# Attention of the first block: a second product of keys and queries in place of transposed scores, with the distances added by the vector engine

## The chip, the cores and the metric

The kernel runs on one NeuronCore of one Trainium2 chip. The metric is the time of one execution on the device in microseconds. TensorE (PE) multiplies into PSUM; VectorE (DVE), ScalarE (ACT) and GpSimd (POOL) work element by element, GpSimd on SBUF alone here; SyncE (SP) issues most DMAs. Each engine works through its own queue in order, and semaphores tie the queues together.

## What is computed

Input x is 8 sequences of 512 tokens with 256 features. Two transformer blocks follow each other; all is float32. Cut to what matters here:

```python
# first block, for each of 8 sequences; H = 16 heads of 16 features
h = layer_norm(x) * (1 + scale) + shift           # from gelu(cond) @ Wt
q, k, v = split(h @ Wqkv)
scores = q @ k.T / 4 - torus_dist * torus_scale[head]
attn = softmax(where(pad, NEG_INF, scores))
x = x + (attn @ v) @ Wout
x = x + gelu(layer_norm(x) @ W1) @ W2
# second block: masked attention without distances, gated by a conditioning vector, and an MLP
```

torus_dist is one 512 x 512 matrix for all sequences, torus_scale one number a head.

## The kernel before

There are 16 passes n: 0 to 7 are the first block's sequences (B = 8), 8 to 15 the second block's. A pass does the attention of sequence n and, between its steps, the dense work of its neighbours: t1 and qk (transposes and projection) of sequence n + 1, v of n itself, and t3, wout, t2, up and down (the rest of the block) of n - 1. The table FIRST says at which step which of these pieces stands, FIRST_DOWN the same for the 32 chunks of the down projection. Three PSUM banks serve the pieces in turn.

The attention of the first block has 32 units of one head and one half (256) of the queries. For a unit u at step k = u (37 steps a pass):

- TensorE, `scores` (line 829): two matmuls of 97 rows, 128 queries by 512 keys. The 97 rows are three terms of 16 split features for two heads, and a mask row. Each goes to one of two score banks.
- VectorE, `shift_scores` (line 1338): adds the scaled distances `bias` to the bank, writes the result to `shifted` and reduces its minimum to `row_max` (signs are turned, so that the minimum stands for the maximum). An instruction that reads the accumulator follows each.
- `bias`, the distances times the head's scale, is made by GpSimd (line 590) for three units in four and by ScalarE (line 1054) for one.
- GpSimd, `subtract_max` (line 597): two subtractions on `shifted`.
- TensorE, `turn_unit` (line 841), two steps later: eight 128x128 transposes, so that keys lie on partitions.
- ScalarE, `exps` (line 1065): two exponentials from PSUM into `probs`.
- TensorE, `attend` (line 856), once for four units: 16 products of probs with `v_ext` (values and a column of ones), 32 instructions.
- ScalarE `take_out` (line 1073), TensorE `to_tokens` (line 865), VectorE `divide` (lines 1359, 1363): the head's output is turned back to tokens and divided by its sum.

A step's order is written out by hand: on TensorE scores, attend, transposes, to_tokens, dense pieces, down chunks; on VectorE division, reductions, dense pieces of the step before, norms. SyncE stores the split q and k to HBM (`store_half`) and loads them back in the layout of the score matmul (`load_group`, a group of four heads in four DMAs). The second block (`pair_scores_of`, `turned_scores_of`) already forms its scores a second time with the maximum in four extra rows; this stays as it is.

## Time and profile before

| | us |
|---|---|
| median of three runs | 1467.23 (1465.11 to 1467.56) |
| the profiled execution, its own time | 1468.33 |
| its span, first to last instruction | 1466.5 |
| TensorE busy | 1307.7 (89%) |
| VectorE busy | 813.6 (55%) |
| ScalarE busy | 771.1 (53%) |
| GpSimd busy | 734.4 (50%) |
| first score product | at 43.8 |
| first score reduction of passes 0, 1, 4, 7 | at 44.78, 129.08, 452.18, 776.21 |
| first reduction of the second block | at 905.23 |

Busy is the time in which an engine has an instruction under way; what stands beside a group of instructions as idle is how long the engine stood still just before them, and what released it. An engine's share over the whole span mixes two blocks, so the rows below are taken from single passes of the first block.

### The profile page before, as it was taken

How to read it: one execution, taken by the hardware profiler on the slowest of the kernel's cores; microseconds unless marked ns; L12 is line 12 of the kernel's file. 1: busy time of each engine (PE TensorE's matmuls, PEld its weight loads, DVE VectorE, ACT ScalarE, POOL GpSimd, SP SyncE). 2: the span in 40 equal slices, each digit the busy share in tenths (PEclk: the TensorE clock that was granted, in tenths of full speed). 3: DMA queues.
4: the chain of work that ended last, by engine and by line, in shares of the span. 5: the costliest groups of instructions: out<-in, count | busy, mean ns of one | idle time of the engine just before them, and what ended most of it. 6: DMA issues, size and time to landing. Idle time of an engine off the chain costs nothing. (4 is left out here: it accounts for less than half of the span.)

```text
span 1466.5 us, 24469 instructions
## 1 busy us (share of the span) xinstructions
PE 1307.7 (89%) x8789; PEld 1006.8 (69%) x8789; DVE 813.6 (55%) x2240; ACT 771.1 (53%) x1262; POOL 734.4 (50%) x885
## 2 busy tenths in 40 slices
PE   4898999999999999999999997888888898887857
PEld 3576777777777777777777775666666666665646
DVE  3766645646646646646646544464565646465451
ACT  3566665665655655755755753454435445452421
POOL 3788876776776776767767751011212213121130
PEclk9999999999999999999999998999999999999878
DMA  8442223223213213313303306262424334241100
GB/s 257 128 127 56 76 77 82 73 65 87 80 51 88 92 40 87 101 31 88 108 23 109 109 23 200 74 205 65 147 76 138 105 110 138 75 144 42 45 15 15
DMA packets 98211, 133.98 MB, mean 91 GB/s; under 512 B 16754, under 2 KB 51450, under 8 KB 98082
## 3 DMA queue, kind: packets, MB, share of 16 engines
q1 hardware_dynamic: 96802, 131.80, 30.2%
q8 instruction: 73, 1.20, 0.4%
q10 hardware_dynamic: 1280, 0.53, 0.1%
q14 instruction: 56, 0.46, 0.1%
HBM read 72.64 MB, written 58.75 MB: 90 GB/s over the span
## 5 line engine op out<-in xcount | busy, mean ns | idle before, releaser
L1338 DVE CUSTOM_DVE_ANT_0 shifted<-score,bias 128x512 f32<-128x512 f32 x512 | 332.8, 688 | 256.0 <-PE score L829 169.3
L597 POOL TENSOR_SCALAR shifted<-shifted,row_max 128x512 f32<-128x512 f32 x512 | 360.1, 716 | 220.8 <-DVE row_max L1338 218.8
L1065 ACT ACTIVATE probs<-turned 128x512 f32<-128x512 f32 x512 | 278.3, 596 | 211.1 <-PE turned L841 209.5
L841 PE MATMUL turned<-ident,shifted 128*128 128x128 f32 x2048 | 269.4, 274 | 6.8 <-POOL shifted L597 6.1
L841 PEld LDWEIGHTS turned<-ident,shifted 128*128 128x128 f32 x2048 | 233.0, 141 | 55.6 <-issue 26.7
L761 PE MATMUL dense<-w_down,hidden 128*128 128x256 f32 x1024 | 251.5, 381 | 0.8 <-ACT hidden L1046 0.8
L590 POOL TENSOR_SCALAR bias<-dist,scale 128x1024 f32<-128x1024 f32 x192 | 219.1, 1142 | 13.6 <-DMA down_bias<-in_L_cond_b 13.6
L829 PE MATMUL score<-k_rows,q_rows 97*128 97x512 f32 x512 | 205.3, 456 | 23.1 <-DVE row_max L1338 10.1
L761 PEld LDWEIGHTS dense<-w_down,hidden 128*128 128x128 f32 x1024 | 184.5, 190 | 32.2 <-issue 9.6
L741 PE MATMUL dense<-feat_m,w_up 128*128 128x512 f32 x768 | 190.1, 403 | 3.4 <-ACT hidden L1046 1.8
L741 PEld LDWEIGHTS dense<-feat_m,w_up 128*128 128x128 f32 x768 | 145.4, 193 | 37.6 <-ACT hidden L1046 5.2
L829 PEld LDWEIGHTS score<-k_rows,q_rows 97*128 97x128 f32 x512 | 92.1, 190 | 66.4 <-DVE row_max L1338 51.9
L856 PE MATMUL pv<-probs,v_ext 128*32 128x256 f32 x2048 | 123.8, 382 | 0.8 <-DVE attn L1363 0.8
L611 POOL CAST mask_colf<-mask_col 128x4 f32<-128x4 uint8 x8 | 1.5, 188 | 238.1 <-PE pv L908 162.2
L1046 ACT ACTIVATE hidden<-dense,up_bias 128x512 f32<-128x512 f32 x128 | 86.3, 689 | 56.9 <-PE dense L741 56.6
L1081 ACT ACTIVATE probs<-turned 128x512 f32<-128x512 f32 x128 | 69.5, 595 | 87.6 <-PE turned L898 60.5
L741 PE MATMUL dense<-feat_a,w_qkv 128*128 128x512 f32 x384 | 109.2, 428 | 2.8 <-DVE feat_a L1292 2.8
L1372 DVE TENSOR_REDUCE row_max<-score 128x8 f32<-128x1024 f32 x64 | 78.2, 1222 | 36.5 <-PE score L879 36.5
L856 PEld LDWEIGHTS pv<-probs,v_ext 128*32 128x32 f32 x2048 | 60.2, 109 | 53.9 <-issue 17.7
L741 PEld LDWEIGHTS dense<-feat_a,w_qkv 128*128 128x128 f32 x384 | 73.9, 204 | 16.6 <-issue 3.2
L579 POOL TENSOR_SCALAR var_eps<-mean_var 128x4 f32<-128x4 f32 x32 | 8.2, 256 | 144.9 <-DVE mean_var L1221 120.1
L1033 ACT ACTIVATE qk_high<-dense 128x512 fp32r<-128x512 f32 x64 | 38.3, 598 | 73.3 <-PE dense L741 71.1
(134 smaller groups left out, 1546.0 us busy)
## 6 DMA issues: line engine op xcount, KB each, us to landing
qk_rows<-qk_high SPq DMA_DIRECT2D x128, 256.0 KB
q_rows<-qk_rows SPq DMA_DIRECT2D x64, 384.0 KB
qk_rows<-qk_low SPq DMA_DIRECT2D x64, 256.0 KB
k_rows<-qk_rows SPq DMA_DIRECT2D x68, 192.0 KB
x_in_t<-in_x SPq DMA_DIRECT2D x8, 512.0 KB, 4.0
x_res<-in_x SPq DMA_DIRECT2D x8, 512.0 KB, 5.4
x_mid<-x_norm SPq DMA_DIRECT2D x8, 512.0 KB, 3.3
x_in_t<-x_mid SPq DMA_DIRECT2D x8, 512.0 KB, 3.9
```

What stands on the lines that cost most here:

```text
L590: pool.tensor_scalar(bias[:, u % 2, :, :], dist[:, 2 * half:2 * half + 2, :], scale[:, h:h + 1], 0.0, ALU.mult, ALU.add).then_inc(s["bias_ ...
L597: ins = pool.tensor_scalar(shifted[:, u % 3, i, :], shifted[:, u % 3, i, :], -1.0, row_max[:, t % 6:t % 6 + 1], ALU.mult, ALU.add)
L741: mm = pe.matmul(out_ap, left, right, start=(i == 0), stop=(i == len(terms) - 1))
L761: mm = pe.matmul(bank_of(piece, m)[:, 0:D], hidden[:, c, P * i:P * i + P], w_down[:, c, :], start=(c == 0), stop=(c == FCH - 1))
L829: pe.matmul(score_bank[t % 2], q_rows[0:KROWS, g % 2, j // 2, q0:q0 + P], k_rows[0:KROWS, g % 2, j // 2, j % 2, :], start=True, stop=True) ...
L841: mm = pe.transpose(turned_bank[z % 2][:, HALF * kk + P * i:HALF * kk + P * i + P], shifted[:, u % 3, i, P * kt:P * kt + P], ident[:, :])
L856: mm = pe.matmul(pv_bank[SLOT * j:SLOT * j + SLOT, 0:HALF], v_ext[:, kt, HG * (gq // 2) + j, :], probs[:, (4 * gq + j) % RING, kt, :], sta ...
L1046: act.activation(hidden[:, i, :], bank[:, :], ACT.Gelu_apprx_tanh if m < B else ACT.Gelu, bias=up_bias[:, i:i + 1]).then_inc(used(piece, m ...
L1065: act.activation(probs[:, u % RING, 2 * pair:2 * pair + 2, :], turned_bank[z % 2][:, :].rearrange("p (a c) -> p a c", a=2), ACT.Exp)\
L1081: act.activation(head_probs[:, h % RING, :], turned_bank[h % 2][:, :], ACT.Exp)\
L1338: dve.tensor_tensor_reduce(shifted[:, u % 3, i, :], score_bank[t % 2], bias[:, u % 2, i, :], 1.0, 3.0e38, ALU.add, ALU.min, row_max[:, t % ...
L1372: dve.tensor_reduce(row_max[:, :].rearrange("p (a t) -> p t a", a=2), pair_scores, mybir.AxisListType.X, ALU.max).then_inc(s["peak_ready"], 1)
```

## The change

In the first block scores are no longer transposed. `first_scores` forms them as before, and `take_minima` reduces their minimum with the distances added, now only for the minimum: the matrix it writes is left over. The minima of a pair of heads (four units) are split in two parts by GpSimd (`split_peaks`), turned by TensorE (piece "peak"), negated and copied by ScalarE, and sent by a DMA from ScalarE's queue into four more rows of `q_rows`. Seven steps (LAG) after its first product a unit gets a second one, `second_scores`, with keys on partitions and the maximum subtracted by these rows. `bias_turned` (VectorE) multiplies the transposed distances `dist_t` by the head's scale, adds the product and writes `key_probs`; with EVICTED = 0 all 32 units go this way, and the branch through `evict` and `add_dist` is used by none. One exponential in place, of 1024 elements, follows (`unit_exp`). A unit is now one head and half of the queries in the first product, and one head and half of the keys in the second. Rows are loaded by pairs of heads (`load_pair`), four DMAs for the first four pairs and three for the others. `subtract_max` and `turn_unit` go from this block. The tables of pieces and chunks are redone, a pass has 42 steps, and the gelus of the steps 13 and 17 are done by ScalarE a step later. The prologue gets a chain of small operations on the scales (`scales`), two small loads ahead of the others, and sixteen transposes of the distances in pass 0.

```diff
--- before.py
+++ after.py
...
-    FIRST = {0: [("v", 0)], 1: [("v", 1)], 2: [("t3", 0), ("t3", 1)], 4: [("v", 2)], 5: [("v", 3), ("t1", 0)],
-             6: [("t1", 1)], 7: [("wout", 0)], 8: [("wout", 1)], 9: [("wout", 2)], 10: [("wout", 3)],
-             11: [("qk", 0)], 12: [("qk", 1)], 13: [("qk", 2)], 14: [("qk", 3)], 15: [("t2", 0), ("t2", 1)],
-             17: [("up", 0), ("up", 1), ("up", 2), ("up", 3)], 21: [("up", 4), ("up", 5), ("up", 6), ("up", 7)],
-             27: [("down", 0)], 30: [("down", 1)], 32: [("down", 2)], 35: [("down", 3)]}
+    FIRST = {0: [("v", 0), ("v", 1)], 1: [("t3", 0), ("t3", 1)], 2: [("v", 2), ("v", 3)],
+             3: [("wout", 0), ("wout", 1)], 4: [("wout", 2), ("wout", 3)], 5: [("peak", 0), ("t1", 0), ("t1", 1)],
+             7: [("qk", 0)], 8: [("qk", 1)], 9: [("peak", 1), ("qk", 2)], 10: [("t2", 0), ("t2", 1)],
+             13: [("peak", 2), ("up", 0), ("up", 1)], 14: [("up", 2), ("up", 3)], 15: [("qk", 3)],
+             17: [("peak", 3), ("up", 4), ("up", 5)], 18: [("up", 6), ("up", 7)], 21: [("peak", 4)],
+             25: [("peak", 5), ("down", 0)], 29: [("peak", 6)], 31: [("down", 1)], 33: [("peak", 7)],
+             35: [("down", 2)], 40: [("down", 3)]}
+
+
+    LAG = 7
+    FIRST_STEPS = UNITS + 10
     STEPS = UNITS + 5
-    FIRST_DOWN = {25: (0, 2), 26: (2, 5), 27: (5, 8), 28: (8, 12), 29: (12, 14), 30: (14, 17), 31: (17, 20),
-                  32: (20, 24), 33: (24, 26), 34: (26, 29), 35: (29, 32)}
-    FIRST_NORM = {2: ("stats", 0), 4: ("norm", 0), 11: ("stats", 1), 13: ("norm", 1)}
-    ADD_BIAS = {14: 0, 15: 1, 16: 2, 17: 3}
+    FIRST_DOWN = {21: (0, 2), 22: (2, 3), 23: (3, 5), 24: (5, 6), 25: (6, 8), 26: (8, 9), 27: (9, 11), 28: (11, 12),
+                  29: (12, 14), 30: (14, 15), 31: (15, 17), 32: (17, 19), 33: (19, 21), 34: (21, 23), 35: (23, 25),
+                  36: (25, 27), 37: (27, 28), 38: (28, 29), 39: (29, 31), 40: (31, 32)}
+    FIRST_NORM = {1: ("stats", 0), 3: ("norm", 0), 6: ("stats", 1), 8: ("norm", 1)}
+    ADD_BIAS = {10: 0, 11: 1, 12: 2, 13: 3}
+    GELU_LATER = (13, 17)
...
+    EVICTED = 0
...
     def bias_by_act(u):
...
+
...
         ab = sb("ab", [P, 2, DC, B])
 
         shifted = sb("shifted", [P, 3, 2, L])
...
+            def load_pair(m, q):
+
+                sp.wait_ge(s[f"halves_stored{q // 4}"], STORED * (m + 1))
+                if q < 4:
+                    sp.wait_ge(s["mask_ready"], m + 1)
+
+                if m > 0 or q > 3:
+                    sp.wait_ge(s["turned_ready"], TILES * m + 8 * (q - 3))
+                loaded = s[f"pair{q % 4}_loaded"]
+                g, pair = row_slot(q)
+                heads = slice(2 * q, 2 * q + 2)
+                sp.dma_start(q_rows[0:MASK_AT, g, pair, :].bitcast(F32),
+                             qk_rows[m, 0, heads, :, :].rearrange("a r n -> (a r) n")).then_inc(loaded, 16)
+                for a in range(2):
+                    sp.dma_start(k_rows[HROWS * a:HROWS * a + HROWS, g, pair, a, :].bitcast(F32),
+                                 qk_rows[m, 1, 2 * q + a, :, :]).then_inc(loaded, 16)
+                if q < 4:
+                    sp.dma_start(k_rows[MASK_AT:KROWS, g, pair, :, :].bitcast(F32),
+                                 mask_neg[:, :].bitcast(F32).unsqueeze(1).broadcast_to([1, 2, L])).then_inc(loaded, 16)
+
...
+                for c in range(3):
+                    store_half(n + 1, c)
+                load_pair(n, 4)
+                load_pair(n, 5)
+                store_half(n + 1, 3)
+                load_pair(n, 6)
+                next_mask(n + 1)
+                load_pair(n, 7)
+                for q in range(4):
+                    load_pair(n + 1, q)
+                if n > 0:
+                    store_y(n - 1)
...
-            def subtract_max(n, u):
-                for i in range(2):
-                    t = 2 * u + i
-                    pool.wait_ge(s["scores_used"], TILES * n + t + 1)
-                    ins = pool.tensor_scalar(shifted[:, u % 3, i, :], shifted[:, u % 3, i, :], -1.0,
-                                             row_max[:, t % 6:t % 6 + 1], ALU.mult, ALU.add)
-                ins.then_inc(s["shifted_ready"], 1)
+                pool.tensor_scalar(bias[:, u % 2, :, :], dist[:, 2 * half:2 * half + 2, :], used_scale[:, n, h:h + 1],
+                                   0.0, ALU.mult, ALU.add).then_inc(s["bias_ready"], 1)
+
+            def split_peaks(n, q):
+
+                pool.wait_ge(s["scores_used"], TILES * n + 8 * q + 8)
+                if q > 0:
+                    piece_ready(pool, ("peak", q - 1), n)
+                elif n > 0:
+                    piece_ready(pool, ("peak", H // 2 - 1), n - 1)
+                low = row_max[:, 8 * (q % 2):8 * (q % 2) + 8].rearrange("p (a t) -> p a t", a=2)
+                parts = split_peak[:, :].rearrange("p (a x t) -> p a x t", a=2, x=2)
+                pool.tensor_copy(parts[:, :, 0, :], low).then_inc(s["first_high"], 1)
+                pool.wait_ge(s["first_high"], H // 2 * n + q + 1)
+                pool.tensor_tensor(parts[:, :, 1, :], low, parts[:, :, 0, :].bitcast(F32), ALU.subtract)\
+                    .then_inc(s["first_split"], 1)
+
...
+                    for k in range(UNITS + 1):
+                        if at(k, SPLIT_AT) is not None:
+                            split_peaks(n, at(k, SPLIT_AT))
                         if k + 2 < UNITS and not bias_by_act(k + 2):
                             make_bias(n, k + 2)
+                        if k >= LAG and evicted(k - LAG):
+                            add_dist(n, k - LAG)
                         if k == 2 and n + 1 < B:
                             inverse_std(n + 1, 0)
-                        if k == 11 and n > 0:
+                        if k == 7 and n > 0:
                             inverse_std(n - 1, 1)
                         if k in ADD_BIAS and n > 0:
                             add_bias(n - 1, ADD_BIAS[k])
-                        if k == 18:
-                            pool.wait_ge(s["bias_ready"], 24 * n + k + 3 - (k + 3) // 4)
+                        if k == 24:
+                            pool.wait_ge(s["first_split"], H // 2 * n + 6)
...
+                if name == "peak":
+                    pe.wait_ge(s["first_split"], H // 2 * m + i + 1)
+                    mm = pe.transpose(bank[0:4 * TT, 0:P], split_peak[:, :].bitcast(F32), ident[:, :])
...
+            def first_scores(n, u):
+                q, a, half = u // 4, u // 2 % 2, u % 2
+                g, pair = row_slot(q)
+                if u % 4 == 0:
+                    pair_loaded(pe, n, q)
+                for i in range(2):
+                    t = 2 * u + i
+                    if n > 0 or t > 1:
+                        pe.wait_ge(s["scores_used"], TILES * n + t - 1)
+                    q0 = HALF * half + P * i
+                    pe.matmul(score_bank[t % 2], q_rows[0:KROWS, g, pair, q0:q0 + P], k_rows[0:KROWS, g, pair, a, :],
+                              start=True, stop=True).then_inc(s["scores_ready"], 1)
...
+            def second_scores(n, w):
+
+                q, a = w // 4, w // 2 % 2
+                g, pair = row_slot(q)
+                if n == 0 and w == 0:
+                    pe.wait_ge(s["row_ones"], 64)
+                    pe.wait_ge(s["dist_t_ready"], TT)
+                if w % 4 == 0:
+                    pe.wait_ge(s["peaks_loaded"], 16 * (H // 2 * n + q + 1))
+                for i in range(2):
+                    if w > 0:
+                        turned_taken(pe, n, w - 1, i)
+                    elif n > 0:
+                        turned_taken(pe, n - 1, UNITS - 1, i)
+                    kt = 2 * (w % 2) + i
+                    pe.matmul(turned_bank[i][:, :], k_rows[:, g, pair, a, P * kt:P * kt + P], q_rows[:, g, pair, :],
+                              start=True, stop=True).then_inc(s["turned_ready"], 1)
...
+            def attend_pair(n, q):
...
+                pe.wait_ge(s["probs_ready"], TILES * n + 8 * q + 8)
...
+                if n < B:
+                    for k in range(FIRST_STEPS):
+                        listed_here = pieces(FIRST, k, n)
+                        for piece, m in listed_here:
+                            if piece[0] == "peak":
+                                dense(piece, m)
+                        if k < UNITS:
+                            first_scores(n, k)
+                        if LAG <= k < LAG + UNITS:
+                            second_scores(n, k - LAG)
+                        if at(k, OUTPUT_AT) is not None:
+                            attend_pair(n, at(k, OUTPUT_AT))
+                        if at(k, TOKENS_AT) is not None:
+                            to_tokens(n, at(k, TOKENS_AT))
+                        if n == 0 and k in (1, 3):
+                            turn_dist(k - 1)
+                            turn_dist(k)
+                        for piece, m in listed_here:
+                            if piece[0] != "peak":
+                                dense(piece, m)
+                        if n > 0 and k in FIRST_DOWN:
+                            down_chunks(n - 1, *FIRST_DOWN[k])
+                    return
...
+                elif name == "peak":
+                    if m > 0 or i > 0:
+                        act.wait_ge(s["peaks_loaded"], 16 * (H // 2 * m + i))
+                    act.activation(peaks[:, :], bank[0:4 * TT, 0:P], ACT.Copy, scale=-1.0).then_inc(used(piece, m), 1)
+                    piece_read(act, piece, m)
+                    g, pair = row_slot(i)
+                    act.dma_start(q_rows[PEAK_AT:ALL_ROWS, g, pair, :].bitcast(F32), peaks[:, :].bitcast(F32))\
+                        .then_inc(s["peaks_loaded"], 16)
...
+            def unit_exp(n, w):
+                h = w // 2
+                if evicted(w):
+                    act.wait_ge(s["dist_added"], EVICTED * n + evicted_before(w) + 1)
+                    factor = used_scale[:, n, h:h + 1]
+                else:
+                    turned_taken(act, n, w, 1)
+                    factor = -1.0
+                act.activation(key_probs[:, w % RING, :, :], key_probs[:, w % RING, :, :], ACT.Exp, scale=factor)\
+                    .then_inc(s["probs_ready"], 2)
...
+                if n < B:
+                    for k in range(FIRST_STEPS):
+                        for piece, m in pieces(FIRST, k, n):
+                            if piece[0] == "peak":
+                                dense(piece, m)
+                        if at(k, TOKENS_AT) is not None:
+                            take_out(n, at(k, TOKENS_AT))
+                        for x in ((k - 1, k) if k - 1 in GELU_LATER else (k,)):
+                            for piece, m in pieces(FIRST, x, n):
+                                if piece[0] != "peak" and x not in GELU_LATER or piece[0] == "up" and x < k:
+                                    dense(piece, m)
+                        if n == 0 and k in (1, 3):
...
+                        if k + 2 < UNITS and bias_by_act(k + 2):
+                            make_bias(n, k + 2)
+                        for w in (k - LAG - 2, k - LAG - 1):
+                            if 0 <= w < UNITS and evicted(w) == (w == k - LAG - 2):
+                                unit_exp(n, w)
...
+            def take_minima(n, u):
+
+                if bias_by_act(u):
+                    dve.wait_ge(s["act_bias_ready"], 8 * n + u // 4 + 1)
+                else:
+                    dve.wait_ge(s["bias_ready"], 24 * n + u + 1 - (u + 2) // 4)
+                for i in range(2):
+                    t = 2 * u + i
+                    dve.wait_ge(s["scores_ready"], TILES * n + t + 1)
+                    dve.tensor_tensor_reduce(left_over[:, i, :], score_bank[t % 2], bias[:, u % 2, i, :], 1.0, 3.0e38,
+                                             ALU.add, ALU.min, row_max[:, t % 16:t % 16 + 1])\
+                        .then_inc(s["scores_used"], 1)
+
+            def bias_turned(n, w):
+                place_free(dve, n, w)
+                h = w // 2
+                for i in range(2):
+                    dve.wait_ge(s["turned_ready"], TILES * n + 2 * w + i + 1)
+                    dve.scalar_tensor_tensor(out=key_probs[:, w % RING, i, :], in0=dist_t[:, 2 * (w % 2) + i, :],
+                                             scalar=used_scale[:, n, h:h + 1], in1=turned_bank[i][:, :],
+                                             op0=ALU.mult, op1=ALU.add).then_inc(s["biased_ready"], 1)
...
+
+                any_key = turned_bank[1][:, 0:B]
+                dve.wait_ge(s["any_turned"], 1)
+                dve.tensor_scalar(query_scale, any_key, QUERY_SCALE[0], None, ALU.mult).then_inc(s["any_ready"], 1)
...
+                if n < B:
+                    for k in range(FIRST_STEPS):
+                        if at(k, DIVIDE_AT) is not None:
+                            divide_pair(n, at(k, DIVIDE_AT))
+                        if k < UNITS:
+                            take_minima(n, k)
+                        if LAG <= k < LAG + UNITS and not evicted(k - LAG):
+                            bias_turned(n, k - LAG)
+                        for piece, m in pieces(FIRST, k - 1, n):
+                            dense(piece, m)
...
+                    divide_pair(n, H // 2 - 1)
...
```

## Rows read from the trace of the kernel before

**Rows 1.** Windows: window, length, busy us (count) PE, PEld, DVE, ACT, POOL; granted clock.
```profile
44.78:129.08 84.30, 78.94 (x652) 57.91 (x651) 54.60 (x170) 53.09 (x93) 72.78 (x91) 0.98 0.39 113
344.51:452.17 107.66, 103.91 (x802) 81.60 (x800) 62.99 (x195) 65.90 (x110) 77.94 (x97) 1.00 0.26 74
...
883.73:905.23 21.50, 13.38 (x68) 11.67 (x68) 9.22 (x24) 4.66 (x8) 1.29 (x2) 0.84 0.82 231
```

**Rows 2.** TensorE's groups by line, window 344.51 to 452.17 (busy, mean ns, idle before).
```profile
L841 PE MATMUL turned<-ident,shifted 128*128 128x128 f32 x256 | 33.7, 274 | 0.9 <-POOL shifted L597 0.9
```

**Rows 3.** VectorE's groups by line, the same window; then line 1338 alone (windows view).
```profile
L1338 DVE CUSTOM_DVE_ANT_0 shifted<-score,bias 128x512 f32<-128x512 f32 x64 | 41.6, 687 | 33.2 <-PE score L829 22.6 <-ACT bias L1054 8.3 <-POOL bias L590 1.8
...
L1194 DVE TENSOR_SCALAR x_norm<-x_in_t,mean_var,rstd 128x256 f32<-128x256 f32 x4 | 2.9, 784 | 0.0
L1299 DVE SCALAR_TENSOR_TENSOR qk_low<-dense,qk_high 128x512 fp32r<-128x512 f32 x4 | 2.7, 687 | 0.0
L1292 DVE TENSOR_TENSOR feat_m<-hidden,feat_m 128x512 fp32r<-128x512 f32 x2 | 2.0, 995 | 0.0
...
L1194 DVE TENSOR_SCALAR x_norm<-x_res,mean_var,rstd 128x256 f32<-128x256 f32 x4 | 1.5, 421 | 0.0
...
L1295 DVE TENSOR_TENSOR feat_m<-dense,feat_m 128x512 fp32r<-128x512 f32 x2 | 1.3, 684 | 0.0
...
344.51:452.17 107.66, 41.85 (x128) 1.00 0.26 74
```

**Rows 4.** ScalarE's groups, the same window; then GpSimd's of the whole span.
```profile
L1065 ACT ACTIVATE probs<-turned 128x512 f32<-128x512 f32 x64 | 34.8, 596 | 26.9 <-PE turned L841 26.6
L1054 ACT ACTIVATE bias<-dist,scale 128x1024 f32<-128x1024 f32 x8 | 9.2, 1150 | 0.0
...
L1046 ACT ACT_TABLE_LOAD x2 | 2.6, 1283 | 0.0
...
L597 POOL TENSOR_SCALAR shifted<-shifted,row_max 128x512 f32<-128x512 f32 x512 | 360.1, 716 | 220.8 <-DVE row_max L1338 218.8
L590 POOL TENSOR_SCALAR bias<-dist,scale 128x1024 f32<-128x1024 f32 x192 | 219.1, 1142 | 13.6 <-DMA down_bias<-in_L_cond_b 13.6
L581 POOL TENSOR_TENSOR rstd<-var_eps,minus_half 128x4 f32<-128x4 f32 x32 | 33.6, 1051 | 2.7
```

**Rows 5.** Timeline, TensorE: start us, duration us, line, operation, count, idle before and releaser.
```profile
444.19 1.04 PE L841 MATMUL turned<-ident,shifted 128*128 128x128 f32 x8
...
445.28 2.32 PE L761 MATMUL dense<-w_down,hidden 128*128 128x256 f32 x10
...
452.92 0.50 PE L829 MATMUL score<-k_rows,q_rows 97*128 97x512 f32 x1 [0.59 <-DVE row_max L1338]
...
910.55 5.68 PE L741 MATMUL dense<-feat_m,w_up 128*128 128x512 f32 x24
```

**Rows 6.** Timeline, VectorE, in the start of the last pass of the first block.
```profile
776.21 0.68 DVE L1338 CUSTOM_DVE_ANT_0 shifted<-score,bias 128x512 f32<-128x512 f32 x1
...
776.82 0.69 DVE L1338 CUSTOM_DVE_ANT_0 shifted<-score,bias 128x512 f32<-128x512 f32 x1
...
783.38 1.28 DVE L1295 TENSOR_TENSOR feat_m<-dense,feat_m 128x512 fp32r<-128x512 f32 x2
```

**Rows 7.** DMA issues: count, KB each, median us to landing.
```profile
x_in_t<-in_x SPq DMA_DIRECT2D x8, 512.0 KB, 4.0
```

**Rows 8.** Timeline of the last attend of a pass and what follows it.
```profile
447.53 1.93 PE L856 MATMUL pv<-probs,v_ext 128*32 128x256 f32 x32
...
449.53 0.39 ACT L1073 ACTIVATE head_out<-pv 128x256 f32<-128x256 f32 x1 [3.62 <-PE pv L856]
...
452.18 0.68 DVE L1338 CUSTOM_DVE_ANT_0 shifted<-score,bias 128x512 f32<-128x512 f32 x1
```

**Rows 9.** Windows view, behind the end of the first block.
```profile
885.20:892.00 6.80, 5.93 (x26) 5.52 (x27) 2.25 (x4) 2.87 (x5) 0.00 (x0) 0.50 0.58 144
```

**Rows 10.** Timeline, VectorE, in the prologue.
```profile
13.93 0.19 DVE L1409 TENSOR_TENSOR tp<-pv,bt_col 128x32 f32<-128x32 f32 x1 [7.08 <-PE pv L924]
```

329 lines of the change are left out of this document (222 added, 107 removed).

## The prediction

> **What bounds the kernel now.** The windows view comes first, cut at the first score reduction of each pass [rows 1]. The first block is one short pass of 84.3 us and seven of 107.6. In these seven TensorE is busy 103.9 of 107.7 us and VectorE 63.0 (one is shown; five others are within 0.2 us of it, one is 1.0 longer). TensorE sets the pace at the full clock; VectorE has 44.7 us to spare. The groups of one such pass [rows 2 to 4] then tell what each engine spends. Mean durations of matmuls overlap, so I price them by what one adds behind its neighbour, from the timeline [rows 5]: eight transposes take 1.04 us with a drain of 0.16, so 0.11 each; 24 matmuls of 512 columns 5.68, so 0.23 each; five down chunks (ten instructions) 2.32, so 0.43 a chunk. An instruction on VectorE that follows another starts 0.61 us after a score reduction and 0.60 after a 128x512 subtraction from PSUM [rows 6].
>
> **The change, part by part** (per pass of the first block, 32 units). I call a 128x512 reduction M (two a unit) and a new 128x512 multiply-add of distances onto the turned product B (two a unit).
>
> TensorE loses 256 transposes, 256 x 0.115 = 29.4 us, and gains 64 second products of the same shape as a score matmul but for four more rows: 64 x 0.23 = 14.8. Eight transposes of the maxima add 1. Net: 103.9 - 29.4 + 14.8 + 1 = about 90 us. That is the gain if TensorE stays the bound.
>
> VectorE keeps 64 M at 0.61 = 39.0 us, its other work, 63.0 less 41.9 that line 1338 takes in that pass [rows 3], = 21.1, and gains 64 B. B has not run here; its nearest row is qk_low, the same scalar_tensor_tensor with one PSUM and one SBUF operand, 687 ns alone and 0.60 us to its successor [rows 3, 6]. So B costs 64 x 0.60 = 38.4 (bounds 0.60 and 0.69: 38 to 44). Sum 98.5.
>
> GpSimd drops 64 subtractions of 716 ns [rows 4]. VectorE operations with both tensors in SBUF run slow while GpSimd is busy: feat_m 995 ns, against 684 with one operand in PSUM; x_norm 784 against 421 [rows 3]. Four x_norm and two feat_m, with two more feat_a, come down by 0 to 2.4 us with GpSimd less busy; I take 0.5, since GpSimd's biases fall in the same steps, so VectorE needs 98.0. The Trainium skill (SBUF — State Buffer, Who interferes with whom) says that a VectorE instruction with two SBUF inputs contends with a GpSimd one that reads SBUF, and one with at most one SBUF input, which B is, does not. By that rule and with a GpSimd that is out of the way the sum would be 8 x 1.9 lower, 1526.
>
> ScalarE turns 64 exponentials of 596 ns into 32 of 1024 elements, priced as its 1024-element copy, 1.15 us [rows 4]: 34.6 to 36.8. Eight small copies and DMA issues of maxima add some 5. It reaches about 75 us and bounds nothing by its sum, but its place in the order matters below. SyncE issues 28 row loads a pass for 16; the loads of a pair are asked for four or more steps ahead, so I cost them at nothing, with 1 us a pass as the other end. The maxima go by DMA three steps (7.3 us) ahead of their use; a 512 KB load lands in 4.0 us [rows 7], so I cost this at nothing as well; if ScalarE were 2 us late each pair would cost up to 1 us, 8 a pass.
>
> So VectorE, 98.0 us, is now the longest queue, over TensorE's 90. Both are in-order, and TensorE can be only one step ahead of VectorE: each score bank and each turned bank is filled again only after VectorE has read it. A step lasts for VectorE 2 M + 2 B = 2.43 us and what stands beside. If R is what TensorE has in a step behind its last second product, the next M can start R + 0.74 us after the last B before (0.50 release to result [rows 5], 0.23 for the next product). A wait comes where R is over 1.7 plus VectorE's extra work. Through the pass:
> - Steps 0 to 6 (no B yet): VectorE has 7 x 1.22 and some 9 of dense work. Step 0 waits 0.8 for two v pieces, step 3 0.3 for GpSimd's root (a bias of 1.14 and 1.4 of small operations, most of it the root's 1.05, stand ahead of it [rows 4]). 1.1 us of waits.
> - Steps 7 to 31: qk pieces (R 1.4) hide. Step 12 (an attend, 1.86) waits 0.1. Steps 13 to 20 carry R of 3.1, 2.8, 1.4, 1.9, 3.1, 2.8, 0 and 1.9 (four up pieces of 6 x 0.23 in each two steps, attends at 16 and 20). The eight gelus are in two groups at ScalarE's steps 14 and 18, each with two table loads of 1.28 [rows 4], and the exponentials of the next two units stand behind: last up product + 0.85 + 1.28 + 2 x 1.15 = 4.4 us, with qk_high and a bias more, while attend needs them in the step after next. Following the two queues from the start of step 13, step 14's M starts at 3.8, 15's at 7.6, 16's at 10.1, 17's at 14.8 (attend had waited 2.0 for its exponentials), 18's at 18.8, 19's at 22.5, 21's at 29.0 (attend waited 1.2). VectorE's own work in this is 8 x 2.43 + 1.8 = 21.2, so 7.8 us of waits. Steps 24 and 28 (attend and a chunk, 2.3) wait 0.6 each. Together 9.1.
> - Steps 32 to 41 (no M): B alone, 1.21 a step, against 0.46 and R of 2.7, 1.2, 0.9, 0.9, 2.7, 0.7, 0.4. TensorE sets these; the last B ends at 14.5. Then a chain that nothing covers: exponential 1.2, attend 1.93 with its start, take_out 0.4, chunk and transposes 0.7, division 0.6: 4.9 us. The trace of before shows its last part, attend at 447.53 to the next M at 452.18 with three chunks in it [rows 8]. 19.4 us, in which VectorE works 11.5: waits of 7.9.
>
> A pass: 98.0 + 1.1 + 9.1 + 7.9 = 116.1 us against 107.6 to 107.8, so +8.4. What goes late next where VectorE has slack is the last B of a unit, then exponential and attend.
>
> Pass 0 has no down, up, wout: VectorE 54.6 - 41.9 + 77.4 = 90.1, waits 1 + 1 + 7, 99 against 84.3: +15. The prologue gets some ten tiny VectorE operations in its 7.1 us of idle time [rows 10], and two DMA issues (0.5 each) ahead, against a first row load half as large: 0, with 1 either way. The stretch behind pass 7 (21.5 us at [rows 1]) and the second block keep their code: 0.
>
> The sum goes against the profiled execution, 1468.3 us (span 1466.5): 1468.3 + 7 x 8.4 + 15 = 1542. This execution was 1.1 over the median of 1467.2, so **1541 us**.
>
> **Rivals.**
> A: the forecast, VectorE bound with waits as counted, 1515 to 1572. For it: the sum of VectorE alone leaves 9.6 us a pass for all waits before the change breaks even in a pass, and the tail alone takes 7.9.
> B: fewer waits. If the surplus of steps 13 to 20 is absorbed (attend and gelus fit), a pass is 98.0 + 1.1 + 1.3 + 7.9 = 108.3: 1467 + 5 + 13 = 1485. Against it: nothing in the order lets TensorE run ahead two steps.
> C, the other side: VectorE runs without a gap but the 4.9 us chain and the small-operand relief comes whole (2.4): 96.1 + 4.9 = 101 a pass, 6.7 less than before; 1467 - 47 + 12 = 1432; it decides once all waits of a full pass are under 7.5 us, since seven passes must each win the 2.1 that pay for pass 0. With less relief and 3 us of waits it is 1450.
> D: TensorE's clock. It fell to half for 6.8 us behind the wait at the end of the first block, and in it TensorE was busy 5.93 us for the work of some 3 [rows 9]. In steps 0 to 12 TensorE would be idle more than anywhere in a full pass of before. If the granted clock falls to 1.2 GHz once a pass with VectorE just keeping up, at most 3.4 us are lost each: 1541 + 8 x 3.4 = 1568; twice a pass, 1595. The Trainium skill (TensorE: Matmul & The Clock Gate, HAM oscillation) says that an engine which waits between bursts of matmuls falls back to the half clock again and again. Where that rule holds here the time is this rival's. Against it: the clock stayed at 1.00 in every full pass of before, and I count no idle stretch of TensorE over 2 us in the steps above.
> E: the maxima or the biases arrive late by 1 us a pair: +8 a pass, 1541 + 64 = 1605.
> That the change doesn't do what it says is no rival of weight: with EVICTED = 0 no unit takes the evicted branch, so every unit pays two B.
>
> **Chances.** A 0.58, B 0.16 (of which 0.04 within 0.2% of 1467), C 0.11, D 0.11, E 0.04. A measurement of this kernel can tell 0.2%. Faster 0.11, same 0.04, slower 0.85. The range leaves out C, the part of B near 1467, the tail of D, and E: 1478 to 1588.
>
> **What would show it.** In a full pass of after: 116 us long; VectorE busy 98, TensorE near 90; spacing of B 0.60; VectorE's idle time ended by TensorE's score and turned products in steps 13 to 20 and at the pass end, 5 us ended by the division's transposes; GpSimd under 40 us; clock 1.00. Wrong if VectorE's busy time is under 90 or a B takes 0.7 and more, if its idle time is under 8 us a pass, or if ScalarE's peaks end the waits.

## The result: 13% slower, and the profile after

The changed kernel takes 1657.11 us (median of four, 1651.31 to 1659.24) against 1467.39 (1465.11 to 1471.11) for the kernel before on the same chip: 1.1282 times, 95% interval 1.1254 to 1.1310. The direction was forecast, the size was not: +190 us for +74, and 1657 lies far over the range's end of 1588.

The page of after, its busy times and the slices that matter (each digit a tenth; PEclk is the granted clock):

```profile
PE 1365.2 (82%) x7335; PEld 919.9 (56%) x7335; DVE 1141.8 (69%) x2764; ACT 778.1 (47%) x1074; POOL 408.8 (25%) x501
...
PE   5787888888888788798888868888888888889767
...
DVE  5887778788788688688788787745564564654452
...
PEclk9777799899899899989989989989999999999888
```

The windows of after: pass 0, then a full pass (pass 4), its five stretches (steps 0 to 6, 7 to 12, 13 to 20, 21 to 31, and 32 to the next pass), and the last stretch before the second block. Columns as in [rows 1]: window, length, busy time (count) of PE, PEld, DVE, ACT and POOL, granted clock.

```profile
45.34:171.01 125.67, 103.07 (x470) 54.28 (x470) 94.96 (x236) 56.02 (x72) 31.76 (x43) 0.69 0.26 79
556.92:686.30 129.38, 109.51 (x618) 70.17 (x617) 102.98 (x259) 66.48 (x86) 37.45 (x49) 0.92 0.20 62
556.92:580.37 23.45, 17.11 (x81) 13.61 (x80) 18.10 (x58) 7.78 (x13) 8.22 (x9) 0.78 0.23 68
580.37:600.92 20.55, 17.87 (x81) 9.96 (x80) 20.24 (x48) 11.25 (x15) 9.35 (x13) 0.84 0.36 118
600.92:632.64 31.72, 27.78 (x158) 18.48 (x157) 22.39 (x55) 23.07 (x29) 8.14 (x11) 0.95 0.20 62
632.64:664.69 32.05, 27.65 (x150) 16.05 (x148) 29.95 (x77) 14.84 (x18) 10.34 (x15) 1.00 0.13 39
664.69:686.30 21.61, 19.10 (x154) 12.06 (x155) 12.30 (x26) 9.54 (x12) 1.40 (x2) 1.00 0.13 38
1075.30:1096.60 21.30, 12.98 (x68) 11.46 (x68) 9.47 (x25) 4.66 (x8) 1.28 (x2) 0.82 0.77 220
```

All of the loss is in the first block. It went from 860.4 us (first reduction at 44.78, second block's at 905.23) to 1051.3 (45.3 to 1096.6), +191; the stretch behind the last pass is 21.3 us, as it was [rows 1]. Pass 0 grew by 41.4 (forecast 15), a full pass by 20 to 22 (forecast 8.4): passes 1 to 6 take 128.7, 127.4, 129.9, 129.4, 129.4 and 129.2.

Where a full pass stands against the forecast; "waits" is the length less VectorE's busy time in the windows above. The prediction states all the waits, and the lengths of the third and the last stretch. The other three forecast lengths share out over the steps, after the result, what is left of its 98.0 us of work; its own words for the first (7 x 1.22, some 9, and 1.1 of waits) would make 18.6.

| steps of pass 4 | forecast | after | VectorE busy | waits, forecast | waits, after |
|---|---|---|---|---|---|
| 0 to 6 | 19.4 | 23.4 | 18.1 | 1.1 | 5.4 |
| 7 to 12 | 19.5 | 20.6 | 20.2 | 0.1 | 0.3 |
| 13 to 20 | 29.0 | 31.7 | 22.4 | 7.8 | 9.3 |
| 21 to 31 | 28.8 | 32.0 | 30.0 | 1.2 | 2.1 |
| 32 to the end | 19.4 | 21.6 | 12.3 | 7.9 | 9.3 |
| pass | 116.1 | 129.4 | 103.0 | 18.1 | 26.4 |

So of the 13.3 us, 5.0 are work of VectorE and 8.3 are waits: 4.3 of them in the head (steps 0 to 6), 2.6 in steps 7 to 31 and 1.4 at the end. The groups of the page behind the work:

```profile
L1594 DVE CUSTOM_DVE_ANT_0 shifted<-score,bias 128x512 f32<-128x512 f32 x512 | 331.5, 684 | 130.6 <-PE score L948 129.8
L691 POOL TENSOR_SCALAR bias<-dist,no_bias 128x1024 f32<-128x1024 f32 x192 | 220.2, 1148 | 702.1 <-DVE row_max L1594 683.9
L1603 DVE SCALAR_TENSOR_TENSOR probs<-shifted,no_bias,turned 128x512 f32<-128x512 f32 x512 | 358.7, 742 | 43.3 <-PE turned L966 42.8
L1290 ACT ACTIVATE probs<-probs 128x1024 f32<-128x1024 f32 x256 | 266.8, 1051 | 110.2 <-DVE probs L1603 109.9
...
L966 PE MATMUL turned<-q_rows,k_rows 101*128 101x512 f32 x512 | 219.3, 479 | 38.3 <-DVE probs L1603 26.2
L948 PE MATMUL score<-k_rows,q_rows 97*128 97x512 f32 x512 | 221.6, 497 | 23.3 <-DVE row_max L1594 15.2
```

M (line 1594) costs what it did [rows 3]. B (line 1603) is 742 ns long, where its nearest row had 687, and its successor comes 0.66 us after it, not 0.60. Counting for each instruction only the time that it adds to VectorE's busy time, the 64 B add 42.9 us to pass 4, where 38.4 was forecast. VectorE waits 130 us for first products and 43 for second ones. TensorE is no longer the full queue of [rows 1]. It is still busy for 109.5 of 129.4 us as modelled, more than VectorE's 103.0; the second products (line 966) alone are 26.6 us of this, where the prediction priced 14.8. A product that stands alone is shown until the end of its drain, so how much of the 109.5 TensorE could have given to other work is not shown.

### The profile page after: what moved, and what is told of

The parts are those of the page before. It is cut to its first block and busy times, and to the rows that moved or that the text cites. A ratio compares the mean times of both kernels' runs of the same rounds, so it can differ in the third digit from the quotient of the medians.

```text
span 1656.7 us, 22196 instructions
## 1 busy us (share of the span) xinstructions
PE 1365.2 (82%) x7335; PEld 919.9 (56%) x7335; DVE 1141.8 (69%) x2764; ACT 778.1 (47%) x1074; POOL 408.8 (25%) x501
## 5 line engine op out<-in xcount | busy, mean ns | idle before, releaser
L691 POOL TENSOR_SCALAR bias<-dist,no_bias 128x1024 f32<-128x1024 f32 x192 | 220.2, 1148 | 702.1 <-DVE row_max L1594 683.9
L1603 DVE SCALAR_TENSOR_TENSOR probs<-shifted,no_bias,turned 128x512 f32<-128x512 f32 x512 | 358.7, 742 | 43.3 <-PE turned L966 42.8
L1290 ACT ACTIVATE probs<-probs 128x1024 f32<-128x1024 f32 x256 | 266.8, 1051 | 110.2 <-DVE probs L1603 109.9
L966 PE MATMUL turned<-q_rows,k_rows 101*128 101x512 f32 x512 | 219.3, 479 | 38.3 <-DVE probs L1603 26.2
L948 PE MATMUL score<-k_rows,q_rows 97*128 97x512 f32 x512 | 221.6, 497 | 23.3 <-DVE row_max L1594 15.2
L966 PEld LDWEIGHTS turned<-q_rows,k_rows 101*128 101x128 f32 x512 | 102.8, 203 | 127.7 <-DVE probs L1603 86.6
L989 PE MATMUL pv<-probs,v_ext 128*32 128x256 f32 x2048 | 148.7, 440 | 21.4 <-ACT probs L1290 21.4
L1267 ACT ACTIVATE bias<-dist,no_bias 128x1024 f32<-128x1024 f32 x64 | 73.4, 1147 | 111.2 <-DVE row_max L1594 111.1
L1317 ACT ACTIVATE probs<-turned 128x512 f32<-128x512 f32 x128 | 69.5, 595 | 87.8 <-PE turned L1077 60.5
L1670 DVE TENSOR_SCALAR peaks<-score 16x128 fp32r<-16x128 f32 x64 | 17.6, 276 | 79.6 <-PE score L1067 71.3
```

The costliest lines, as they stand in the source:

```text
L691: pool.tensor_scalar(bias[:, u % 2, :, :], dist[:, 2 * half:2 * half + 2, :], used_scale[:, n, h:h + 1], 0.0, ALU.mult, ALU.add).then_inc( ...
L948: pe.matmul(score_bank[t % 2], q_rows[0:KROWS, g, pair, q0:q0 + P], k_rows[0:KROWS, g, pair, a, :], start=True, stop=True).then_inc(s["sco ...
L966: pe.matmul(turned_bank[i][:, :], k_rows[:, g, pair, a, P * kt:P * kt + P], q_rows[:, g, pair, :], start=True, stop=True).then_inc(s["turn ...
L989: mm = pe.matmul(pv_bank[SLOT * c:SLOT * c + SLOT, 0:HALF], v_ext[:, kt, 2 * q + a, :], key_probs[:, (4 * q + 2 * a + kt // 2) % RING, kt % 2,
L1267: act.activation(bias[:, u % 2, :, :], dist[:, 2 * half:2 * half + 2, :], ACT.Copy, scale=used_scale[:, n, h:h + 1]).then_inc(s["act_bias_ ...
L1290: act.activation(key_probs[:, w % RING, :, :], key_probs[:, w % RING, :, :], ACT.Exp, scale=factor)\
```

## The experiments

Each ratio is to the kernel before on the same chip; before was 1466.1 to 1469.6 us beside these runs. "Against after" is the difference of two medians from different chips: by the ratios e1_imm, for one, is 16 us under after and not 21. A difference from 1.1282 under about 0.005 can't be told from none by the totals. The last column is the length of the first block in the one profiled execution, from its first M to the second block's first reduction; what follows it has the same code in all these kernels and still took 555 to 565 us, which is a good part of the spread of the totals. Three kernels leave something of the result out: e3_small and e10_small_order the distances and the second product in 480 of 512 columns of each B, e11_nogelu the nonlinearity.

| | us | ratio (95%) | against after | first block |
|---|---|---|---|---|
| after | 1657.1 | 1.1282 (1.1254 to 1.1310) | | 1051.3 |
| e1_imm: B's factor a constant | 1636.1 | 1.1174 (1.1127 to 1.1221) | -21 | 1032.8 |
| e2_warm: first products twice, steps 0 to 12 | 1665.2 | 1.1364 (1.1321 to 1.1406) | +8 | 1059.4 |
| e3_small: B on 32 columns | 1551.1 | 1.0589 (1.0549 to 1.0629) | -106 | 943.3 |
| e4_evict12: 12 of 32 units by ScalarE and GpSimd | 1798.0 | 1.2255 (1.2210 to 1.2300) | +141 | 1195.5 |
| e5_head: dense pieces first, steps 0 to 6 | 1651.0 | 1.1241 (1.1197 to 1.1285) | -6 | 1044.3 |
| e6_out: output ahead of the maxima's copy | 1644.6 | 1.1189 (1.1145 to 1.1232) | -13 | 1037.8 |
| e7_warm0: pass 0, all products twice | 1649.5 | 1.1250 (1.1197 to 1.1302) | -8 | 1040.3 |
| e9_all: e1, e5, e6, e7 | 1616.4 | 1.1005 (1.0963 to 1.1046) | -41 | 1005.6 |
| e10_small_order: e3, e5, e6 | 1524.0 | 1.0383 (1.0357 to 1.0409) | -133 | 910.8 |
| e11_nogelu: no gelu tables | 1650.9 | 1.1255 (1.1223 to 1.1286) | -6 | 1044.5 |
| e12_exp1st: exponentials ahead of gelus | 1658.6 | 1.1284 (1.1252 to 1.1317) | +1 | 1055.1 |
| e13_tokens: turn back one step later | 1626.9 | 1.1070 (1.1039 to 1.1102) | -30 | 1024.2 |
| e14_orders: e5, e6, e7, e13 | 1625.6 | 1.1050 (1.1018 to 1.1082) | -31 | 1017.8 |
| e15_tokens_imm: e1, e13 | 1604.7 | 1.0932 (1.0906 to 1.0959) | -52 | 999.3 |
| e16_three: e1, e7, e13 | 1606.4 | 1.0948 (1.0916 to 1.0980) | -51 | 998.1 |

**VectorE's work: how much of the loss is B, and why B costs 0.66.** Two kernels: B's factor as a constant, and B on 32 of its 512 columns (with one memset in the prologue besides).

```diff
 e1_imm
-  scalar=used_scale[:, n, h:h + 1], in1=turned_bank[i][:, :],
+  scalar=0.1, in1=turned_bank[i][:, :],
 e3_small
-  dve.scalar_tensor_tensor(out=key_probs[:, w % RING, i, :], in0=dist_t[:, 2 * (w % 2) + i, :],
+  dve.scalar_tensor_tensor(out=key_probs[:, w % RING, i, 0:32], in0=dist_t[:, 2 * (w % 2) + i, 0:32],
   ...
-  in1=turned_bank[i][:, :],
+  in1=turned_bank[i][:, 0:32],
```

> The changed kernel with one edit: the multiply-add on VectorE (B) takes the scale as a constant (0.1, the value of every head in these inputs) and not from a per-partition column; the second product's maxima and all else stay. The changed kernel took 1657 us; its B started its successor 0.66 us later, where a subtraction without a column takes 0.60. Theory (the column costs 0.058 us an instruction, and VectorE's queue sets the pace): B falls to 0.60, VectorE's busy time in a full pass from 103.0 to 99.3, and the time by 512 x 0.058 = 30 us to about 1627. Rival 1 (the column costs nothing, B is slow for another reason such as two operands): B stays at 0.66 and the time at 1657. Rival 2 (the waits between the queues set the pace and take up the gain): B falls to 0.60 and the time by under 10 us.

> The changed kernel with VectorE's multiply-add B cut to 32 of its 512 columns, in every unit, so that the distances and the second product reach only these columns of the probabilities (that part of the attention is left out); the count of instructions, the order and all semaphores stay, and one memset of 2048 columns is added in the prologue. Theory (VectorE's work in B makes the kernel slow): B takes about 0.15 us in place of 0.66, VectorE's busy time in a full pass falls by 64 x 0.5 = 32 us to 71, TensorE becomes the bound at its 90 us of work plus waits, a full pass is 98 to 104 us in place of 129, and the time is 1400 to 1460, under the kernel before (1467). Rival (the longer chain of a unit, first product, maxima, DMA, second product, exponential, and the waits in it set the pace, whatever B costs): a full pass stays over 115 us and the time over 1550.

The same pair stands within after itself. VectorE's qk_low (line 1557), one tile's view; durations are minimum, median and maximum. `no_bias` among the inputs marks the column of scalars (`query_scale`), the others have a constant:

```profile
L1557 DVE SCALAR_TENSOR_TENSOR qk_low<-dense,qk_high x48: 657/688/693, 28.7 to 1492.0; 128x512 fp32r<-128x512 f32 x48
L1557 DVE SCALAR_TENSOR_TENSOR qk_low<-dense,no_bias,qk_high x16: 736/744/753, 26.8 to 851.2; 128x512 fp32r<-128x512 f32 x16
```

And B of e1_imm, its group by line and its full pass 4:

```profile
L1603 DVE SCALAR_TENSOR_TENSOR probs<-shifted,turned 128x512 f32<-128x512 f32 x512 | 327.9, 681 | 46.8 <-PE turned L966 45.2
```
```profile
551.11:677.66 126.55, 106.30 (x618) 68.18 (x617) 99.13 (x260) 66.53 (x86) 37.53 (x49) 0.95 0.21 64
```

The column costs 61 ns an instruction (742 less 681; to the successor 0.60 us in place of 0.66), 3.9 us of work a pass (103.0 to 99.1). The time fell by 21 us (first block: 18.5) of the 31 that this is in eight passes, between its theory of 30 and its second rival of under 10; the rest went into waits. B in e3_small costs next to nothing, and still its full pass is 115.7 us long with VectorE busy 73:

```profile
502.86:618.60 115.74, 97.11 (x616) 68.14 (x615) 73.12 (x260) 65.87 (x86) 36.95 (x49) 0.96 0.22 70
```

That is 8 us over the pass of before with VectorE's addition nearly gone; the theory (98 to 104 us a pass, 1400 to 1460) fell and the rival (over 115, over 1550) held. So I had the wrong bound in part: without the 30 us of B there remains something, TensorE's work and in-order waits, that alone is nearly as long as my forecast of the whole pass.

**Which waits.** TensorE's in pass 4 of after (who waited for whom: us in total, times, longest):

```profile
PE pv L1046 <- ACT head_out L1309: 4.8, 6, 1.3
PE turned L966 <- DVE probs L1603: 3.0, 15, 0.5
PE pv L989 <- ACT probs L1290: 2.5, 3, 1.2
PE dense L859 <- DVE feat_m L1552: 2.3, 1, 2.3
PE score L948 <- DVE row_max L1594: 1.8, 4, 0.8
PE dense L859 <- DVE x_res L1565: 1.7, 1, 1.7
PE dense L867 <- DVE x_res L1565: 1.7, 1, 1.7
```

Line 1046 turns the attention output back and waits for ScalarE's eviction of it. The timeline of one such place (start, duration; idle before and what ended it):

```profile
643.16 1.04 ACT L1290 ACTIVATE probs<-probs 128x1024 f32<-128x1024 f32 x1
...
644.11 0.25 ACT L1244 ACTIVATE peaks<-dense 16x128 fp32r<-16x128 f32 x1
...
644.39 0.64 ACTq L1247 DMA_DIRECT2D q_rows<-peaks  x1
...
645.13 0.38 ACT L1309 ACTIVATE head_out<-pv 128x256 f32<-128x256 f32 x1 [0.77 <-ACT peaks L1244]
...
645.56 0.44 PE L1046 MATMUL pv<-ident,head_out 128*128 128x128 f32 x2 [0.64 <-ACT head_out L1309]
```

attend ends near 643.2, but ScalarE has an exponential, the copy of the maxima and 0.64 us of issuing their DMA ahead of the 0.38 us eviction. TensorE stands, and its next score products behind it. Three kernels change orders only: e5_head, e6_out and e13_tokens.

```diff
 e5_head, VectorE
+  if k < LAG:
+      for piece, m in pieces(FIRST, k - 1, n): dense(piece, m)
   if k < UNITS: take_minima(n, k)
   ...
-  for piece, m in pieces(FIRST, k - 1, n): dense(piece, m)
+  if k >= LAG:
+      for piece, m in pieces(FIRST, k - 1, n): dense(piece, m)
 e6_out, ScalarE
+  if at(k, TOKENS_AT) is not None: take_out(n, at(k, TOKENS_AT))
   ...  (copy of the maxima, their DMA)
-  if at(k, TOKENS_AT) is not None: take_out(n, at(k, TOKENS_AT))
 e13_tokens, TensorE (and the division on VectorE one step later)
-  if at(k, TOKENS_AT) is not None: to_tokens(n, at(k, TOKENS_AT))
+  if at(k, TOKENS_AT + 1) is not None: to_tokens(n, at(k, TOKENS_AT + 1))
+  if k == FIRST_STEPS - 1: to_tokens(n, H // 2 - 1)
```

> In steps 0 to 6 of each pass VectorE reads the two dense banks of the step before ahead of its four minima, no longer behind them; nothing else moves. If TensorE's in-order waits for these banks (2.31 us at v2, 1.73 at wout, 1.70 at t1 in pass 4) are what makes the head of a pass long, the eighth step's first minimum comes at 19 to 21 us in the place of 23.4 and the time falls by 15 to 30 us, to 1627 to 1642. Rival: the minima then come late themselves and TensorE waits for its score banks in the place of the dense banks: within 5 us of 1657.

> ScalarE evicts the attention output of a unit ahead of the copy of the maxima and of their DMA's issue, where it came behind both. If TensorE's turn back of that output, which stands in its queue ahead of the next score products, sets the pace through its waits of 0.6 to 1.3 us, a full pass is 3 to 5 us shorter and the time 1617 to 1632. Rival: the later maxima row makes the second products wait instead, or the waits only change their name: within 6 us of 1657.

> TensorE turns the attention output back one step later for the first seven pairs of heads of a pass, behind the score products of that step, and VectorE divides one step later; ScalarE's order stays. TensorE then has the output ready when it comes to it: its waits of 0.6 to 1.3 us for it, seven a pass, go, where the order of ScalarE's work took only a part of them (13 us off in all). If these waits pass on to VectorE in full, 7 x 0.8 x 8 = 45 us go; if only those in steps 13 to 20 do, where VectorE already waits, 15 to 25: 1632 to 1642. Rival: VectorE's queue hides them, and the division, now behind a later product, is awaited by the next attend: within 5 us of 1657 or slower.

e5_head: the eighth step's first M comes at 22.0 us in five of the seven full passes, where after has 22.4 to 23.9 in six of them: as its theory had in direction but not in size (19 to 21). Pass 0 became 2.5 us longer. Its head in pass 4, and what TensorE waits for in it:

```profile
559.16:581.18 22.02, 15.86 (x78) 12.15 (x77) 18.21 (x57) 7.66 (x13) 7.29 (x9) 0.82 0.25 73
```
```profile
PE score L948 <- DVE row_max L1594: 4.0, 2, 3.8
PE dense L859 <- DVE feat_m L1552: 1.1, 1, 1.1
PE dense L859 <- DVE x_res L1565: 0.6, 1, 0.6
```

The waits for dense banks fell from 5.7 to 1.7 us and one of 3.8 us for a score bank took their place: the rival's mechanism holds for most of it. The total's -6 can't be told from none.

e6_out brought 13 us, under its theory's 25 to 40 and over its rival's 6; e13_tokens brought 30, the largest effect of a pure order, between the 45 of waits passed on in full and the 15 to 25 of those in steps 13 to 20 alone. Both kernels take the wait at line 1046 away almost whole. Over the whole span, of after, e6_out and e13_tokens:

```profile
PE pv L1046 <- ACT head_out L1309: 35.9, 47, 1.6
```
```profile
PE pv L1046 <- ACT head_out L1309: 1.7, 5, 0.5
```
```profile
PE pv L1046 <- ACT head_out L1311: 0.5, 1, 0.5
```

So the wait itself doesn't tell the two apart. As the mean of passes 1 to 6, both shorten steps 13 to 20 (31.3 us in after, 29.3 and 29.5) and the end (21.7; 20.5 and 20.4), but e6_out lengthens steps 21 to 31 from 32.1 to 33.1, e13_tokens doesn't. Why it does was not followed; it is less than half of the 17 us between the two. Windows of e13_tokens: pass 4 and the same five stretches.

```profile
544.34:669.42 125.08, 108.49 (x618) 69.22 (x617) 103.89 (x260) 66.17 (x86) 36.85 (x49) 0.93 0.21 65
544.34:566.82 22.48, 16.31 (x81) 12.71 (x80) 18.96 (x58) 7.77 (x13) 7.68 (x9) 0.82 0.24 71
566.82:587.21 20.39, 17.51 (x81) 9.34 (x80) 20.25 (x47) 11.09 (x15) 9.34 (x13) 0.87 0.36 113
587.21:617.03 29.82, 27.58 (x158) 18.91 (x157) 22.40 (x56) 23.02 (x29) 8.12 (x11) 0.94 0.22 70
617.03:649.09 32.06, 28.05 (x150) 16.08 (x148) 29.94 (x77) 14.85 (x18) 10.31 (x15) 1.00 0.13 39
649.09:669.42 20.33, 19.04 (x154) 12.19 (x155) 12.33 (x27) 9.45 (x12) 1.40 (x2) 1.00 0.15 41
```

Its waits are 3.5, 0.1, 7.4, 2.1 and 8.0 us, 21.2 in all against 18.1 forecast and 26.4 in after. From step 7 on they are 17.7 for my 17.0. TensorE's turn back in front of its next score products, with the wait at line 1046, is the term that my account of these steps had left out.

**The gelus.** In steps 13 to 20 I had let attend wait for exponentials behind the gelus and their table loads. Two kernels test it: no table loads at all, and the exponentials ahead of the gelus.

```diff
 e11_nogelu, ScalarE
-  act.activation(hidden[:, i, :], bank[:, :], ACT.Gelu_apprx_tanh if m < B else ACT.Gelu,
+  act.activation(hidden[:, i, :], bank[:, :], ACT.Identity if m < B else ACT.Gelu,
 e12_exp1st, ScalarE: the "up" pieces of steps 13 and 14, and of 17 and 18
-  ahead of make_bias and unit_exp of their step
+  behind them
```

> ScalarE's gelus in the first block are plain copies with the bias (the nonlinearity is left out), so that no table is loaded between them and the exponentials: 4 x 1.28 = 5.1 us less of ScalarE a pass, all in steps 13 to 20, which took 31.7 us for 29.0 forecast. If the gelus with their table loads, standing ahead of the exponentials that attend waits for, make these steps long, they take 27 to 29 and the time falls by 20 to 35, to 1622 to 1637. Rival: what stretches these steps is what TensorE issues behind the second products (up pieces, attend at half clock): within 6 us of 1657.

> In the steps of the two groups of gelus, ScalarE does the unit's exponential and its bias ahead of the gelus in the place of behind them; the gelus keep their tables. If attend's wait for probabilities (1.01 and 0.34 us in pass 4) is the cause, steps 13 to 20 shrink by about 1.4 us a pass: 10 us off, 1647. Rival: the dense banks then come free a gelu later, TensorE's up pieces wait for them and the scores behind: 5 to 20 us slower than 1657.

Steps 13 to 20 of pass 4, first of e11_nogelu, then of e12_exp1st:

```profile
600.87:629.55 28.68, 26.45 (x158) 18.20 (x157) 22.40 (x55) 16.56 (x22) 8.11 (x11) 1.00 0.21 62
```
```profile
603.39:636.09 32.70, 27.84 (x156) 18.63 (x157) 22.48 (x57) 22.88 (x28) 8.14 (x11) 0.95 0.21 66
```

ScalarE's work there fell from 23.1 to 16.6 us. The stretch is 3 us shorter in this pass, but only 1.5 as the mean of passes 1 to 6 (29.8 for 31.3), and the total fell by 6, not 20 to 35. The theory that the gelus set these steps fell. The order of ScalarE around them changed nothing in the total (e12_exp1st), but it did not take away the wait that it was meant to take either: attend's wait for probabilities in this stretch is 1.8 us, in after 1.4. So this kernel tests the order and not the wait. What the forecast counted there (2.0 and 1.2 us of attend waiting) was 1.01 and 0.34 in after; that term was too large, and it hid part of the one that was missing.

**TensorE's clock.** The granted clock is 0.78 in the head of pass 4, 0.84 in the next stretch, and 0.69 over the whole of pass 0 (a share of (1 - 0.69) x 2 = 0.62, some 78 us, at 1.2 GHz, where 2.4 is full). Two kernels give TensorE more to do in its gaps without giving anyone more to wait for than these products: e2_warm in steps 0 to 12 of each pass, e7_warm0 in pass 0 alone.

```diff
 e2_warm: first products, u < 13;  e7_warm0: first and second products, n == 0
+  for again in range(2):
+      mm = pe.matmul(...)
-  pe.matmul(...).then_inc(s["scores_ready"], 1)
+  mm.then_inc(s["scores_ready"], 1)
```

> The changed kernel with each first score product of the first 13 units of a pass issued twice into the same bank: nothing of the result changes, TensorE gets 26 more matmuls of 512 columns a pass, 26 x 0.23 = 6 us at the full clock. In the changed kernel the granted clock was at 1.2 GHz for 14 to 24 us of each full pass, nearly all in steps 0 to 12, and for 78 us of pass 0. Theory (the half clock costs time there, and idle stretches of TensorE brought it): the clock stays up in steps 0 to 12, a full pass loses 3 to 6 us, pass 0 five or more, the time falls by 25 to 55 us to 1600 to 1630. Rival 1 (the clock is half only where TensorE waits anyway, the waits for banks set the pace): the clock rises and the time stays within 10 us of 1657 or goes up by up to 8 x 6 = 48 us through the added work. Rival 2: the clock does not rise at all, and the added work at half clock costs up to 8 x 12 = 96 us.

> In pass 0 alone every first and second score product is issued twice; the output is the same. If the half clock, which TensorE has for 77 us of that pass, is what makes pass 0 long (it ran 125.7 us, 27 over the forecast), it goes to full clock and the pass takes 104 to 110 us: the time falls by 15 to 20 us, to 1637 to 1642. Rival: the clock rises or stays and the pass keeps 122 to 128 us, since VectorE and the chain of waits set it: within 4 us of 1657.

The head and the whole of pass 4 in e2_warm, then pass 0 of e7_warm0:

```profile
561.36:584.07 22.71, 16.99 (x101) 13.42 (x99) 18.09 (x58) 7.73 (x13) 8.21 (x9) 1.00 0.24 71
...
561.36:691.39 130.03, 109.84 (x644) 71.14 (x643) 103.01 (x260) 66.36 (x86) 37.36 (x49) 0.97 0.20 62
```
```profile
45.50:164.24 118.74, 104.26 (x594) 62.92 (x595) 95.29 (x235) 55.24 (x71) 31.69 (x43) 0.94 0.27 83
```

In e2_warm the clock is full in this head, which is 0.7 us shorter, but over passes 1 to 6 the heads are 0.6 us longer as a mean (23.8 for 23.2) and the passes 0.8. So half clock in steps 0 to 12 costs a full pass less than the 26 extra products do, whose work is 6 us at most (26 x 0.23). In pass 0 the full clock brings 7 us, net of the extra products: 118.7 for 125.7. Whether this reaches the total is open: e7_warm0 is 8 under after within overlapping intervals and under its theory's 15 to 20, e16_three not under e15_tokens_imm.

**Do they add?** Four kernels combine the changes.

> The three changes of this call together, with the factor of the biased scores as a constant in the place of the column of scalars (which alone took 21 us off). If the terms are separate waits of one chain they add: 21 + 15 to 30 + 25 to 40 + 15 to 20, so 1546 to 1581. If VectorE's stream is the bound once the waits are gone, a pass stops at its 99 us busy plus some 15: not under 1560. If they are one wait under several names the time is that of the best one alone: 1615 to 1636.

> The kernel with B on 32 of its 512 columns (it leaves out the distances, the second products and so the probabilities of the other columns; it took 1551) together with the two changes of order: dense pieces ahead of the minima in steps 0 to 6, and the attention output evicted ahead of the copy of the maxima. With VectorE at 73 us a pass nothing but the in-order waits of TensorE is left. If they are the same waits that the two orders shorten in the full kernel (6 and 13 us off), the time falls by 15 to 25, to 1526 to 1536. If without VectorE's load they are all that bounds a pass, it falls by 35 to 55 to 1496 to 1516. Rival: the load of TensorE itself, 97 to 100 us busy as the trace models it, is the bound and the orders bring nothing: 1546 to 1556.

> All changes of order together, nothing left out: dense pieces first in the head (6 off alone), attention output ahead of the maxima's copy (13 off), the turn back a step later, and the doubled products of pass 0 (8 off). If they are separate waits: 1657 - 27 - 5 to 15 more for the turn back, 1615 to 1625. If the turn back's step and ScalarE's order take the same wait, 1628 to 1635. If TensorE's load outside waits is the bound, not under 1645. None of the theories expects it under the 1467 of the kernel before, since VectorE is busy for 103 us of each pass of 107.7.

> The turn back of the attention output one step later (30 us off alone) together with the constant in the place of B's column of scalars (which leaves out the scale of the distances; 21 off alone). In the first of these VectorE waits 21 us a pass and works 103 to 104; the constant takes 3.9 of the work. If what is left of a pass is VectorE's work and the waits that the forecast had counted, a full pass is 121 to 122.5 and the time 1596 to 1606. Rival: as before, TensorE's queue takes the gain back in waits for score products and the time is not under 1612.

> The same two changes and every score product of pass 0 issued twice (8 off alone), so that TensorE keeps the full clock there. If the clock of pass 0 is a cost of its own, 6 to 9 us under the kernel with the two changes: 1588 to 1600. Rival: pass 0 is as long as with two (its waits then come from the order alone): within 3 us of that kernel.

e9_all is 41 under after for 48 as the plain sum of its four parts as measured; its first expectation, 1546 to 1581, had assumed them larger. At 1616.4 it lies in the range for one wait under several names (1615 to 1636), though it is 20 us under the best of its parts alone. e10_small_order shows the orders alone, with VectorE out of the way: 27 us for the 19 that they bring in the full kernel, between what its first two theories said; VectorE's load may cover some of these waits in the full kernel. e14_orders, 1625.6, lies just outside the ranges of its first two theories (to 1625, and from 1628): with the turn back moved, the other orders and the clock of pass 0 add nothing that the totals show (1.1050 for 1.1070; the first block is 6 us shorter in the profiled executions). e6_out and e13_tokens take the same wait from two ends, and e14's pass 0 has a head of 22.1 us for 18.2. e15_tokens_imm met its own, 1604.7 in 1596 to 1606: B's price and the turn back add in full. Its pass 4, then its pass 0 and that of e16_three:

```profile
532.50:655.66 123.16, 107.18 (x618) 68.59 (x617) 99.96 (x259) 66.15 (x86) 37.01 (x49) 0.94 0.21 66
45.40:165.85 120.45, 97.79 (x471) 52.20 (x471) 90.92 (x235) 55.34 (x71) 31.66 (x43) 0.76 0.27 82
```
```profile
45.53:158.47 112.94, 98.86 (x597) 62.07 (x598) 91.14 (x236) 55.23 (x71) 31.71 (x43) 0.97 0.28 88
```

e16_three's pass 0 is again 7.5 us shorter at the full clock, and its seven later passes are 6.3 us longer in sum (pass 1 alone 3.6). Its expectation of 6 to 9 us off the total failed.

**The other way to add the distances.** The kernel has a branch in which ScalarE evicts a unit and GpSimd adds the distances. It takes B's work from VectorE.

```diff
-  EVICTED = 0
+  EVICTED = 12
```

> The changed kernel with its own constant EVICTED at 12 in place of 0: of the 32 units of a pass 12 are evicted by ScalarE (two copies of 512 columns with a scale) and get their distances from GpSimd (one subtraction of 1024 elements), the other 20 as before by VectorE. Theory (VectorE's queue sets the pace, GpSimd and ScalarE have room: 71.7 and 61.5 us idle of 129): VectorE's busy time in a full pass falls by 12 x 1.32 = 16 us to 87, GpSimd's rises by 12 x 2.4 = 29 to 66, ScalarE's by 12 x 1.2 = 14 to 80, and a pass falls by 10 to 16 us: 1530 to 1575 us in all. Rival (the order of the queues sets the pace): the longer way of an evicted unit makes attend wait and the time stays within 30 us of 1657.

Its pass 4, and what GpSimd's addition costs:

```profile
632.31:779.04 146.73, 112.11 (x619) 72.26 (x618) 89.90 (x236) 80.62 (x110) 65.38 (x61) 0.88 0.18 55
```
```profile
L712 POOL TENSOR_TENSOR probs<-probs,shifted 128x1024 f32<-128x1024 f32 x96 | 228.7, 2382 | 196.8 <-ACT probs L1279 196.8
```

And TensorE's longest wait in that pass:

```profile
PE turned L966 <- ACT probs L1279: 17.2, 9, 4.2
```

VectorE works 13 us less a pass and the pass is 17 longer: neither theory (1530 to 1575, or within 30 us of 1657) had this. Three engines in a row (0.68 x 2 for the eviction, 2.4 for the addition, 1.14 for the exponential) now stand between the second product and attend, but attend waits only 1.2 us for probabilities in this pass. What stands out is TensorE's second product: it waits 17.2 us until ScalarE has evicted the turned banks (line 1279). Work moved off VectorE lost by the wait for the engine that took it.

## Why the prediction was wrong, step by step

- **VectorE's work with waits on top sets the pass, and the kernel loses: right in direction.** That VectorE is the longest queue is not shown: TensorE is busy 109.5 us as modelled, and without nearly all of B the pass is still 115.7 (e3_small). VectorE 103.0 us of work for 98.0, a pass of 129.4 for 116.1, GpSimd 37.5 (under 40 was said), the prologue and the transition at nothing (first M at 45.3 for 44.8, last stretch 21.3 for 21.5).
- **M at 0.61 us: right, but taken out and put back in two ways of counting.** The sum takes 41.9 us for line 1338 out, its busy time, and puts 39.0 back, its spacing; for the pass of before this would make 60.1 where 63.0 was measured. M adds 39.9 to pass 4 of after, so 0.9 of the 5.0 us are here.
- **B at 0.60 us: the term was mis-sized**, inside its bounds of 0.60 to 0.69. The row that I took it from [rows 3, 6] has its factor as a constant, B a column of scalars, and I passed over this difference. Measured 0.66; with a constant 0.60 (681 ns). It is 4.5 us of a pass's work (42.9 for 38.4) and 21 us of the total (e1_imm; 16 by the ratios). The Trainium skill (VectorE: DVE Perf Modes, Scalar operands) names the two kinds, a constant in the instruction and an operand read per partition; here they differ by 61 ns.
- **GpSimd's relief, 0.5 us: too small, inside its 0 to 2.4.** The four x_norm, two feat_m and two feat_a of a pass took 6.8 us in the pass of before that was read and 5.7 in pass 4 of after, 1.1 less. VectorE's other work is 20.2 us (103.0 - 42.9 - 39.9, the last being M) for 20.6 forecast. B itself takes 741 ns beside a working GpSimd (305 of them) and 742 without (207), as the Trainium skill's rule said that I weighed (SBUF — State Buffer, Who interferes with whom). I had left out that the rule makes an exception of VectorE's 2-port perf modes: x_norm has one SBUF tensor as input, and the one of four in each pass that starts just behind a bias of GpSimd takes 1.22 us, the others 0.39 to 0.42, though GpSimd works beside them too. The rest of the 1.9 us a pass that I worked out from that rule did not come; GpSimd's biases still stand beside these instructions.
- **"One step ahead, R + 0.74": the step that failed.** R was to be what TensorE *has to do* behind its last second product. I summed its matmuls and let it wait only for score banks, turned banks and exponentials. It also waits in order for everything else that it reads or writes over: the output that ScalarE evicts behind a DMA issue (4.8 us in pass 4; moving its turn back a step later gave 30 of the 116 missing us, e13_tokens, while taking the wait alone away gave 13, e6_out), and the three dense banks that VectorE reads behind four reductions (5.7 us in the head, seen in the trace of after; an order that takes 4 of them away gets them back as a wait for score banks, e5_head). I had take_out as 0.4 us once, in the tail, and none of it in steps 13, 17 and so on.
- **The gelus in steps 13 to 20: over-counted.** 3.2 us of attend's waits forecast, 1.35 seen, 6 us at most in the total.
- **TensorE at 90 us: not seen as such.** It is busy 109.5 in the model of the profile and 97 to 99 with B small. A product that stands alone shows more busy time (0.49 us in the timeline, to the end of its drain) than the 0.23 that I priced from a run of 24 [rows 5]. Whether this price was wrong, or only the drain shows, no run here tells.
- **Rival D, half clock: right as an event, wrong in its price.** The clock fell in every pass, for 20 us of pass 4 and 78 of pass 0, while I had given it 0.11. I priced at most 3.4 us a fall. In full passes more clock brought no time net of the products that bought it (e2_warm), in pass 0 7 us. The Trainium skill (TensorE: Matmul & The Clock Gate, HAM oscillation) was right here that an engine which waits between bursts keeps falling back; its count of half the throttled time as lost gives an estimate of 32 us for the 64 us that e7_warm0 took away, and the trace shows 7, net of the doubled products.
- **Pass 0 at 99: the thinnest step.** Measured 125.7. Work 95.0 for 90.1 is B's price again. Waits 30.7 for the 9 that I wrote down without following the queues: 3.2 in steps 0 to 6, 5.3 in 7 to 12 (where TensorE waits 3.5 once for the maxima's DMA), 9.0 in 13 to 31, 13.2 at the end. The clock is 7 of it. The rest, some 15 us, was not taken apart.
- **The prediction's list of signs** had the right ones for being wrong: "a B takes 0.7 and more" (0.66 to its successor, 742 ns long), and a clock under 1.00. "5 us ended by the division's transposes" did not hold as said: VectorE's wait at the end of pass 4 is 3.9 us and ended by a down chunk (line 879), and the transposes end 0.2.

Of the 116 us by which the forecast was missed, 21 are B's price and 30 the turn back, both clear of the spread of the runs. The head, the clock in pass 0 and the gelus gave 6 to 8 each, none of them distinguishable from nothing in the total by itself. With the first two out (e15_tokens_imm, 1604.7), 64 us are left over 1541: 21 in pass 0 and about 6 in each later pass (the mean of passes 1 to 6 is 122.5 for 116.1), of which 1.5 are work and 3.4 the head's waits. **These 64 us are located but not explained: their cause stays open.** No kernel of the study beats the one before; even with B on 32 columns and both orders of e10_small_order the time is 1.038 times that of before.

## What to carry to other kernels

When a queue is called full or empty by its sum, its in-order waits are not yet counted: go through each instruction of the queue that stands ahead of the critical one, and for each ask on which engine the last reader or writer of its buffers stands, and behind what. A cheap operation (here a 0.38 us eviction behind a 0.64 us DMA issue) that feeds an engine's head of queue is a term of the sum. If work is moved from the full queue to another that must answer within the same step, price the step as a chain first, and ask which bank stays taken meanwhile. Try to move the consumer a step later, which here was worth 30 us for a few lines. And take a price from a row with the same kinds of operands, the scalar's too.

## What the runs showed of the hardware

- A `scalar_tensor_tensor` of 128x512 with one PSUM and one SBUF operand takes 742 ns with its factor in a column of one value a partition and 681 to 688 with a constant, for two different lines of the kernel: about 60 ns, 8%, each time.
- VectorE's 742 ns instruction with one operand in PSUM ran at the same speed beside GpSimd and without it. Of the four 128x256 `tensor_scalar` x_norm<-x_in_t on SBUF in each of the passes 1 to 6 of after, the one that starts 0.07 us behind the start of GpSimd's bias (1.14 us) takes 1.22 us and ends 0.15 us after it; the others take 0.39 to 0.42.
- TensorE ran at 1.2 GHz for 78 us of a 126 us pass in which the trace models it as busy for 103. Taking 64 of these 78 us away by issuing every score product twice shortened the pass by 7 us.
- Issuing the DMA of 8 KB kept ScalarE for 0.64 us, 0.77 from the end of the copy to the next instruction.
